# ScalarE copies the causal mask into the score banks of a latent attention

## The chip, the cores and the metric

The kernel runs on one core of one Trainium2 chip. The metric is the device time of one launch in microseconds, the median of several runs. TensorE (PE) has a weight queue of its own (PEld), and beside it work VectorE (DVE), ScalarE (ACT), GpSimd (POOL) and the DMA queues, of which SyncE (SP) issues most. Each engine runs its own program in order and meets the others only in semaphores.

## The reference, cut to what matters

The program computes one layer: a cross attention of 16x64 query rows to 16x1601 context rows, a relative attention, then a latent attention and a mixture of experts. The change is in the latent attention (`mla`), which runs over 16 sequences of 64 tokens with 16 heads:

```
kk = concat([k, k_rope]);  qq = concat([q, q_rope])          # 16 + 16 values a head
scores = einsum('bqhd,bkhd->bhqk', qq, kk) * scale
causal = tril(ones((S, S)))
scores = where(causal, scores, finfo.min)
probs  = softmax(scores)
y      = einsum('bhqk,bkhd->bqhd', probs, v) @ W_o
```

## The kernel before, in words

The 1024 tokens are eight blocks of 128 rows, two sequences each. A block has 16 heads x 64 keys of scores a row, which fill two PSUM banks: bank 4 for heads 0 to 7 (half f=0) and bank 5 for heads 8 to 15 (f=1).

The blocks are pipelined by hand in `self_step(k)`, which every engine has in its own version. The steps k=1 to 4 stand in a hardware loop, and 0, 5, 6 and 7 are written out. In step k TensorE works on four blocks at once, in this order: it transposes the queries of block k+1 (`query_columns`, L905), the first half of block k's weights (`weight_columns`, L940), makes the latents of block k+2 (`latents`, L872), transposes the keys of block k+1 (`key_columns`, L905) and the second half of the weights (L940), makes the rotary keys (L878), then the scores of block k+1 for f=0 (`self_scores`, L924 and L930), the output of block k (`self_output`, L950), the products from the latents of block k+2 (L882, L885, L898), the scores for f=1 (L924 and L930), transposes of block k+3 (L863) and the output product of block k (L960 to L962). Steps 6 and 7 have no further blocks to make latents of.

`self_scores` starts each half with one bf16 product of an identity (`ident_bf`) and the mask (`causal_bf`, eight copies of a 64-column mask, 0 or -1e30), 128 rows x 512 columns, which begins the sum in the bank. Four products of queries and keys add to it; each writes one half of the partitions (`bank[4 + f][own, ...]`). The mask product waits until the exponentials of the block before have read the bank (`sexp_ready`), and the products of queries and keys wait for the spread keys (`kTh_ready`).

ScalarE's `self_step(k)` moves the queries' columns out (`queries_columns_out`, L1608), the first half of the transposed weights (`weights_out`, L1628), spreads two of four parts of the keys (`keys_spread`, two copies, L1391), takes the eight exponentials of f=0 (`self_exps`, L1621), moves out what came from the latents (`heads_out`, L1594 to L1602), and takes the eight exponentials of f=1. In step 0 the order is keys_spread, weights_out, and then one cast of an expert's weights (L1657). VectorE spreads the other two parts of the keys (L1391, DVE), moves out the second half of the weights, splits two pieces of expert weights in the loop's steps (L2191), and takes the negated row maximum of each half (`self_max`, L2161 and L2163), on which the exponentials wait. Between the two maxima lie the casts of the attention's output (L2177, L2179), the norm of a later block and one reciprocal (`self_inv`, L2169). GpSimd multiplies the exponentials with the reciprocal sums (L1287).

Two more places are touched. In the relative attention, GpSimd clears `hn4` (L1262) and later `pos_g` (L1268); VectorE's first `group_turned` waited for the first of these, `attT_cleared`. The mask tile is made by VectorE long before (L2072).

Of the kernel before, what the change touches and what calls it, by code (L numbers as in the profile page):

```python
# [128 lines left out]
def perceiver_kernel(nc, x, ctx_keys, consts, vecs, rows, Wq, Wv, Wr, Wout, Wkvd, Wqd, Wku, Wqu, Wvu, Wropeq, Wropek,  # L129
                     Wo, Wexp, Wrouter, out):  # L130
    with ExitStack() as ctx:
        def sem(name):
            return ctx.enter_context(nc.semaphore(name))

        def sbuf(scope, name, shape, dt=F32):
            return scope.enter_context(nc.sbuf_tensor(name, shape, dt))
# [3 lines left out]
        bank = [ctx.enter_context(nc.psum_tensor(f"bank{i}", [P, 512], F32)) for i in range(8)]  # L140
# [16 lines left out]
        ident_bf = sbuf(ctx, "ident_bf", [P, P], BF16)  # L157
# [5 lines left out]
        hn4 = sbuf(ctx, "hn", [P, 4, D])  # L163
# [30 lines left out]
        def place(kb, name, shape, dt=F32):  # L194

            with ExitStack() as below:
                if kb:
                    sbuf(below, f"{name}_below", [P, int(kb * 256)])
                return sbuf(below, name, shape, dt)
# [47 lines left out]
        causal_bf = place(151, "causal_bf", [P, 8, SQ], BF16)  # L247
# [67 lines left out]
        pos_loaded = sem("pos_loaded")  # L315
        hg_act, hg_dve, ku_ready, v_full, v_out, con_full, con_out = (sem(n) for n in ("hg_act", "hg_dve", "ku_ready", "v_full", "v_out", "con_full", "con_out"))
        abias_ready, exp_ready, ainv_ready, att_ready = (sem(n) for n in ("abias_ready", "exp_ready", "ainv_ready", "att_ready"))
        attT_cleared, pos_cleared, attT_ready, o_full, o_act, o_dve = (
            sem(n) for n in ("attT_cleared", "pos_cleared", "attT_ready", "o_full", "o_act", "o_dve"))
        ohi_ready, olo_ready = sem("ohi_ready"), sem("olo_ready")  # L320
        bout_added, y2_full, y2_ready = sem("bout_added"), sem("y2_full"), sem("y2_ready")

        mla_loaded, raw_loaded = sem("mla_loaded"), sem("raw_loaded")
        causal_ready, cleared, xn_ready, xnT_full, xnT_ready = (sem(n) for n in ("causal_ready", "cleared", "xn_ready", "xnT_full", "xnT_ready"))
        lat_full, lat_ready, k_full, vv_full, q_full = (sem(n) for n in ("lat_full", "lat_ready", "k_full", "vv_full", "q_full"))
        raw_ready, vv_ready, kq_ready, qTh_full, kTh_full = (sem(n) for n in ("raw_ready", "vv_ready", "kq_ready", "qTh_full", "kTh_full"))
        qTh_ready, kTh_ready, self_full, sbias_ready, sexp_ready = (sem(n) for n in ("qTh_ready", "kTh_ready", "self_full", "sbias_ready", "sexp_ready"))
# [47 lines left out]
        def own_values(t, half):  # L375

            at = slice(0, 34 * HD) if half == 0 else slice(HD, 31 * HD)
            blocks = t[SQ * half:SQ * (half + 1), at].rearrange("p (b r d) -> p b r d", b=2, d=HD)
            return blocks[:, :, 0:2 * PAIRS - 1:2, :]
# [167 lines left out]
        def _(pe):  # L547
# [370 lines left out]

            def self_scores(t, par, halves):
                for f in halves:  # L920
                    if not (isinstance(t, int) and t == 0):
                        pe.wait_ge(sexp_ready, 2 * t + f - 1)

                    nc.tensor.matmul(bank[4 + f][:], ident_bf[:], causal_bf[:].rearrange("p n q -> p (n q)"), start=True,  # L924
                                     stop=True)
                    pe.wait_ge(kTh_ready, 2 * t + 2)
                    for i in range(2):
                        for b in range(2):
                            own = slice(SQ * b, SQ * (b + 1))
                            last = nc.tensor.matmul(bank[4 + f][own, i * D // 2:(i + 1) * D // 2], qT_h[par][:, 2 * f + i, own],  # L930
                                                    kT_h[par][:, 2 * f + i, 4 * b:4 * b + 4, :].rearrange("p n q -> p (n q)"),
                                                    start=False, stop=True, skip_group_check=True)
                    last.then_inc(self_full, 1)
# [154 lines left out]
            for j in range(NJ):  # L1088
# [13 lines left out]
                elif j == 4:  # L1102
# [5 lines left out]
                    for k in range(1, NT):  # L1108
                        nc.tensor.matmul(bank[3][:, k * NE:NT * NE], ones_bf[:], picks[:, 0:(NT - k) * NE], start=False,
                                         stop=True, skip_group_check=True)  # L1110

                    for k in range(NT):
                        last = nc.tensor.matmul(bank[3][:, NT * NE:(NT + 1) * NE], ones_bf[:], r_picks[:, k, :], start=k == 0,
                                                stop=k == NT - 1, skip_group_check=True)
# [92 lines left out]
            with pe.Fori(0, TILES // 2 - 2) as i:  # L1207
                at = places_of(2 * i + 2, 3)
                for n, par in enumerate((1, 0)):
                    t = 2 * i + 4 - par  # L1210
# [17 lines left out]
        def _(pool):  # L1228
# [30 lines left out]
            nc.gpsimd.tensor_tensor(y[:], y[:], bout_sb[:].unsqueeze(1).broadcast_to([P, NT, D]),  # L1259
                                    ALU.add).then_inc(bout_added, 1)  # L1260
            pool.wait_ge(hT_full, NT)
            nc.gpsimd.memset(hn4[:], 0.0).then_inc(attT_cleared, 1)  # L1262
            pool.wait_ge(kT_act, NH)
            pool.wait_ge(kT_dve, NH)
            group_queries(0, 0)
# [123 lines left out]
        def head_keys_out(copy, par, h):  # L1389
            rows_h = slice(HD * h, HD * (h + 1))  # L1390
            return copy(kT_h[par][rows_h, :, KEY_PLACES[h], :], bank[3][rows_h, :].rearrange("p (c b q) -> p c b q", c=QUADS, b=2))  # L1391

        @block.scalar
        def _(act):
# [194 lines left out]
            def heads_out(k, par):  # L1589
                act.wait_ge(k_full, k + 1)  # L1590
                kr = bank[2][:].rearrange("p (a h d) -> p a h d", a=2, d=RD)
                if not (isinstance(k, int) and k == 0):
                    act.wait_ge(kq_ready, k)
                nc.scalar.copy(raw[:, 0:HEADS, :], kr[:, 0])  # L1594
                nc.scalar.copy(kq[par][:, 0:HEADS, 0:RD], kr[:, 1])
                act.wait_ge(q_full, k + 1)
                qr = bank[1][:].rearrange("p (a h d) -> p a h d", a=2, d=RD)
                nc.scalar.copy(kq[par][:, HEADS:, 0:RD], qr[:, 0])
                nc.scalar.copy(raw[:, HEADS:, :], qr[:, 1]).then_inc(raw_ready, 1)
                act.wait_ge(vv_full, k + 1)  # L1600
                for half in range(2):
                    last = nc.scalar.copy(own_values(v_own[par], half),  # L1602
                                          bank[3][SQ * half:SQ * (half + 1), :].rearrange("p (b r d) -> p b r d", b=2, d=HD))
                last.then_inc(vv_ready, 1)

            def queries_columns_out(k, par):
                act.wait_ge(qTh_full, k + 1)
                nc.scalar.copy(qT_h[par][:].rearrange("p c q -> p (c q)"), bank[3][:]).then_inc(qTh_ready, 1)  # L1608

            def keys_spread(k, par):  # L1610
                act.wait_ge(kTh_full, k + 1)
                for h in range(2):
                    last = head_keys_out(nc.scalar.copy, par, h)
                last.then_inc(kTh_ready, 1)

            def self_exps(k, par, halves):
                for f in halves:
                    act.wait_ge(sbias_ready, 2 * k + f + 1)
                    for n in range(8):
                        h = 8 * f + n  # L1620
                        last = nc.scalar.activation(sp_[par][:, h, :], bank[4 + f][:, n * SQ:(n + 1) * SQ], ACT.Exp,  # L1621
                                                    bias=s_bias[par][:, h:h + 1], scale=SELF_SCALE,
                                                    accum_out=s_sum[par][:, h:h + 1])
                    last.then_inc(sexp_ready, 1)

            def weights_out(k):
                act.wait_ge(spT_full, 2 * k + 1)
                nc.scalar.copy(spT[:, 0:4, :].rearrange("p n q -> p (n q)"), bank[6][:]).then_inc(spT_act, 1)  # L1628

            def self_step(k, par, scores=True, project=True):  # L1630
                first = isinstance(k, int) and k == 0
                if scores and not first:
                    queries_columns_out(k + 1, 1 - par)
                if first:
                    keys_spread(1, 1)
                weights_out(k)
                if scores and not first:
                    keys_spread(k + 1, 1 - par)
                elif not scores:
                    expert_columns_out(0)  # L1640
                    expert_columns_out(1)
                    for t in range(4):
                        columns_high(t)
                if isinstance(k, int) and k == 0:
                    act.wait_ge(raw_loaded, 4 * 16)
                    high_part(up)
                if scores:
                    self_exps(k + 1, 1 - par, (0,))
                if project:
                    heads_out(k + 2, par)  # L1650
                if scores:
                    self_exps(k + 1, 1 - par, (1,))
# [12 lines left out]
            def columns_high(k):  # L1665
                act.wait_ge(xf_act if k < 2 else xf_ready, k + 1 if k < 2 else k - 1)
                nc.scalar.copy(xT_hi[:, :, k * P:(k + 1) * P], xf[k % 4][:]).then_inc(xhi_ready, 1)
# [7 lines left out]
            queries_columns_out(0, 0)  # L1675
            keys_spread(0, 0)
            heads_out(1, 1)
            self_exps(0, 0, range(2))
            self_step(0, 0)
            with act.Fori(0, NT // 2 - 2) as i:  # L1680
# [96 lines left out]
        def _(dve):  # L1777
# [253 lines left out]
            group_low(3, 1)  # L2031
            group_max(1, 1)
            group_inv(0, 0)
            dve.wait_ge(attT_cleared, 1)
            group_turned(0, 0)
            for g in range(NG - 2):
                group_max(g + 2, g % 2)
# [422 lines left out]
            with dve.Fori(0, TILES // 2 - 1) as i:  # L2460
                for par in range(2):
                    t = 2 * i + 1 + par
# [48 lines left out]
```

## Time and profile before

| | |
|---|---|
| median of 3 runs | 825.94 us (825.93 to 828.04) |
| the profiled execution | 827.49 us |
| its span, first to last instruction | 825.7 us |
| mean granted TensorE clock | 0.997 of full |
| TensorE busy | 792.1 us |
| VectorE, ScalarE, GpSimd busy | 523.7, 311.3, 301.0 us |

The times are device microseconds. Of the profiled execution 1.8 us lie outside the span. A row of the timeline gives the start, the duration, the engine, the source line, what it writes and reads, the shapes and the number of instructions merged, and in brackets the idle time before it with what ended it. TensorE's products are pipelined, so the distance from one start to the next tells more than the duration. An fp32 product shows as two or more records.

### The profile page before, as it was taken

Reading aid. Unit: us, or ns where it says so; the run is one execution under the profiler, and the core shown is the slowest. Engines: PE = TensorE matmul, PEld = TensorE weight load, DVE = VectorE, ACT = ScalarE, POOL = GpSimd, SP = SyncE. Lnnn points to the kernel's source line nnn. Section 1 sums busy time; section 2 is a strip of 40 time slices with the busy share of each in tenths; the row PEclk is TensorE's granted clock in tenths of the full one; section 3 lists DMA queues with packets and bytes.
Section 4 is the critical chain, followed back from the end, with each engine's and each line's share of the span. In section 5 each row is a group of like instructions: output and inputs, shape, how many; then the busy total and the mean of one; then the engine's idle time right before and its main releaser. Section 6 shows DMA issues by size and latency. Waiting matters only on the chain.

```text
span 825.7 us, 16716 instructions
## 1 busy us (share of the span) xinstructions
PE 792.1 (96%) x6414; PEld 582.8 (71%) x6415; DVE 523.7 (63%) x1175; ACT 311.3 (38%) x827; POOL 301.0 (36%) x157
## 2 busy tenths in 40 slices
PE   4899999999989999999999999999999999999996
PEld 3555455555547778878876777688888888888883
DVE  5879777977755346776788877855473433343334
ACT  4312331233153427853267756723422112211211
POOL 0000000000062843543022222443639999993033
PEclk9999999999999999999999999999999999999999
DMA  9968556855502013040189000040475464541147
GB/s 342 382 238 319 201 207 234 319 205 208 211 32 103 1 51 106 3 128 7 53 287 375 3 0 0 2 153 1 178 275 204 159 203 155 185 143 51 55 119 259
DMA packets 46573, 127.00 MB, mean 154 GB/s; under 512 B 4001, under 2 KB 8353, under 8 KB 40369
## 3 DMA queue, kind: packets, MB, share of 16 engines
q1 hardware_dynamic: 36752, 105.44, 35.1%
q10 hardware_dynamic: 7200, 12.32, 4.3%
q0 software_dynamic: 2560, 8.39, 3.1%
q8 instruction: 44, 0.72, 0.4%
q14 instruction: 17, 0.13, 0.0%
HBM read 101.99 MB, written 24.15 MB: 153 GB/s over the span
## 4 chain that ended last, share of the span: by engine, by line
PE 78%; DVE 8%; DMA 6%; POOL 3%; ACT 2%; issue 2%; SPq 1%; another core or an unknown queue 0%; DVEq 0%; ACTq 0%; POOLq 0%
PE scores L592 11%; PE bank L625 8%; PE bank L1128 7%; PE bank L1130 7%; PE bank L1129 6%; DMA nat<-in_ctx_keys 5%; DVE ctxT L1820 2%; PE bank L682 2%; POOL picked L1370 2%; PE bank L836 2%; PE bank L684 2%; PE bank L683 2%; PE bank L842 2%; PE bank L837 2%; PE bank L872 2%
## 5 line engine op out<-in xcount | busy, mean ns | idle before, releaser
L1820 DVE STREAM_TRANSPOSE ctxT<-nat 128x1024 f32<-128x1024 f32 (+3 forms) x124 | 116.9, 1005 | 4.1 <-DMA nat<-in_ctx_keys 3.7
L625 PE MATMUL bank<-nat,probT 128*64 128x512 f32 (+1 forms) x416 | 94.4, 597 | 0.1
L592 PE MATMUL scores<-ctxT,hn 32*64 32x385 f32 (+5 forms) x2048 | 88.6, 487 | 3.5 <-DVE ctxT L1820 2.5
L1235 POOL TENSOR_TENSOR wq_lo<-wq_raw,wq_hi 128x1024 fp32r<-128x1024 f32 x4 | 9.5, 2402 | 223.3 <-ACT wq_hi L1461 223.3
L1357 POOL TENSOR_TENSOR ring_lo<-ring_raw,ring_hi 128x2048 fp32r<-128x2048 f32 x18 | 83.0, 4612 | 15.1 <-ACT ring_hi L1708 14.0
L592 PEld LDWEIGHTS scores<-ctxT,hn 32*64 32x64 f32 x2048 | 65.1, 131 | 24.2 <-issue 12.9
L1128 PE MATMUL bank<-ring_hi,xg_lo 128*128 x180 | 74.2, 412 | 0.4 <-DVE xg_lo L2440 0.4
L1130 PE MATMUL bank<-ring_hi,xg_hi 128*128 x180 | 70.6, 392 | 0.0
L1129 PE MATMUL bank<-ring_lo,xg_hi 128*128 x180 | 70.1, 389 | 0.0
L625 PEld LDWEIGHTS bank<-nat,probT 128*64 128x64 f32 (+1 forms) x416 | 28.8, 136 | 52.9 <-issue 51.4
L2452 DVE TENSOR_TENSOR rhm_lo<-bank,rhm_hi 128x512 fp32r<-128x512 f32 x21 | 14.5, 693 | 79.5 <-ACT rhm_hi L1719 75.9
L1725 ACT COPY hn<-bank 128x512 f32<-128x512 f32 x22 | 12.9, 587 | 113.8 <-PE bank L1130 106.9
L1355 POOL TENSOR_TENSOR ring_hi<-ring_raw,cst 128x2048 fp32r<-128x2048 f32 x15 | 54.1, 3604 | 0.0
L1621 ACT ACTIVATE sp<-bank,s_bias 128x64 f32<-128x64 f32 x128 | 38.1, 326 | 21.7 <-DVE s_bias L2163 21.6
L1287 POOL TENSOR_TENSOR sp<-sp,s_inv 128x512 f32<-128x512 f32 x16 | 16.8, 1051 | 80.2 <-DVE s_inv L2169 80.2
L1397 ACT ACTIVATE qn<-y,nmr,rstd 128x2048 f32<-128x2048 f32 x8 | 16.8, 2094 | 61.7 <-DVE nmr L1882 61.7
L1130 PEld LDWEIGHTS bank<-ring_hi,xg_hi 128*128 128x128 f32 x180 | 33.8, 188 | 7.8
L2435 DVE TENSOR_SCALAR xg_hi<-bank,vec 128x128 fp32r<-128x128 f32 x88 | 24.8, 346 | 21.8 <-PE bank L1138 21.5
L1128 PEld LDWEIGHTS bank<-ring_hi,xg_lo 128*128 128x128 f32 x180 | 33.9, 188 | 6.2 <-issue 0.6
L1129 PEld LDWEIGHTS bank<-ring_lo,xg_hi 128*128 128x128 f32 x180 | 34.0, 189 | 5.9
L1370 POOL DMA_INDIRECT picked<-y_slots,slots x16 | 15.8, 986 | 50.3 <-POOLq L1364 44.2
L1128 PE MATMUL bank<-ring_hi,rhm_lo 128*128 x84 | 32.8, 390 | 0.0
(310 smaller groups left out, 1881.4 us busy)
## 6 DMA issues: line engine op xcount, KB each, us to landing
nat<-in_ctx_keys SPq DMA_DIRECT2D x48, 1024.0 KB, 7.6
ring_raw<-in_Wexp SPq DMA_DIRECT2D x21, 1024.0 KB, 6.2
x_slots<-zeros SPq DMA_DIRECT2D x1, 5632.0 KB, 17.6
y_slots<-zeros SPq DMA_DIRECT2D x1, 5632.0 KB, 32.3
hn<-x_slots ACTq DMA_DIRECT2D x22, 256.0 KB, 4.2
y_slots<-hn ACTq DMA_DIRECT2D x22, 256.0 KB
w_raw<-in_Wexp SPq DMA_DIRECT2D x3, 1024.0 KB, 5.3
nat<-in_ctx_keys SPq DMA_DIRECT2D x16, 130.0 KB
```

Of the source, the lines that this page charges most:

```text
L592: last = nc.tensor.matmul(scores4[64 * b:64 * b + 64, i, 0:keys_in[i]], q4[rows_i, j, 64 * b:64 * b + 64], ctxT[rows_i, b, j, 0:keys_in[i] ...
L625: last = nc.tensor.matmul(bank[7][64 * b:64 * b + 64, :], probT[0:n, j, 64 * b:64 * b + 64], nat[k % 2][0:n, b, j, :], start=j == 0, stop= ...
L1128: nc.tensor.matmul(b[:], x_lo[:, c, :], hi, start=c == 0, stop=False)
L1129: nc.tensor.matmul(b[:], x_hi[:, c, :], lo, start=False, stop=False)
L1130: last = nc.tensor.matmul(b[:], x_hi[:, c, :], hi, start=False, stop=c == HC - 1)
L1287: nc.gpsimd.tensor_tensor(sp_[par][:, at, :], sp_[par][:, at, :], s_inv[par][:, at].unsqueeze(2).broadcast_to([P, 8, SQ]), ALU.mult).then_ ...
L1355: nc.gpsimd.tensor_tensor(ring_hi[at], ring_raw[at], zero, ALU.add).then_inc(split_hi, 1)
L1357: last = nc.gpsimd.tensor_tensor(ring_lo[at], ring_raw[at], ring_hi.bitcast(F32)[at], ALU.subtract)
L1370: nc.gpsimd.indirect_dma_start(picked[2 * k + i][:], None, y_slots, bass.IndirectOffsetOnAxis(slots[:, k, i:i + 1], 0)).then_inc(picked_lo ...
L1621: last = nc.scalar.activation(sp_[par][:, h, :], bank[4 + f][:, n * SQ:(n + 1) * SQ], ACT.Exp, bias=s_bias[par][:, h:h + 1], scale=SELF_SCALE,
L1820: dve.transpose(dst, src).then_inc(columns_ready, 1)
L2435: last = dve.tensor_scalar(xg_hi[par][:, c, :], columns[c], weights[c], None, ALU.mult)
```

## The change

For blocks 1 to 7, ScalarE copies the mask into bank 4 and bank 5 (`scores_seeded`), each after its own exponentials have read the bank, and TensorE's products of queries and keys add to what stands there. The 14 mask products of these blocks are gone; TensorE waits for `seeded` in their place. In ScalarE's step the two copies stand after weights_out and before keys_spread (in step 0: before keys_spread, which stands first). Block 0 keeps its two mask products. ScalarE gets a wait for the mask tile ahead of its first exponentials. A semaphore is given up: VectorE's first `group_turned` waits for `pos_cleared`, the later of the two clearings.

```
             def self_scores(t, par, halves):
                 for f in halves:
-                    if not (isinstance(t, int) and t == 0):
-                        pe.wait_ge(sexp_ready, 2 * t + f - 1)
-
-                    nc.tensor.matmul(bank[4 + f][:], ident_bf[:], causal_bf[:].rearrange("p n q -> p (n q)"), start=True,
-                                     stop=True)
+                    if isinstance(t, int) and t == 0:
+                        nc.tensor.matmul(bank[4 + f][:], ident_bf[:], causal_bf[:].rearrange("p n q -> p (n q)"), start=True,
+                                         stop=True)
+                    else:
+                        pe.wait_ge(seeded, 2 * t + f - 1)
                     pe.wait_ge(kTh_ready, 2 * t + 2)
...
-            nc.gpsimd.memset(hn4[:], 0.0).then_inc(attT_cleared, 1)
+            nc.gpsimd.memset(hn4[:], 0.0)
...
+            def scores_seeded(k):
+                for f in range(2):
+                    act.wait_ge(sexp_ready, 2 * k + f + 1)
+                    nc.scalar.copy(bank[4 + f][:], causal_bf[:].rearrange("p n q -> p (n q)")).then_inc(seeded, 1)
+
...
                 if first:
+                    scores_seeded(k)
                     keys_spread(1, 1)
                 weights_out(k)
                 if scores and not first:
+                    scores_seeded(k)
                     keys_spread(k + 1, 1 - par)
...
             heads_out(1, 1)
+            act.wait_ge(causal_ready, 1)
             self_exps(0, 0, range(2))
...
-            dve.wait_ge(attT_cleared, 1)
+            dve.wait_ge(pos_cleared, 1)
             group_turned(0, 0)
```

## Rows read from the trace of the kernel before

**Rows 1.** The page: each engine's busy time, and the chain that ended last.
```profile
PE 792.1 (96%) x6414; PEld 582.8 (71%) x6415; DVE 523.7 (63%) x1175; ACT 311.3 (38%) x827; POOL 301.0 (36%) x157
...
PE 78%; DVE 8%; DMA 6%; POOL 3%; ACT 2%; issue 2%; SPq 1%; another core or an unknown queue 0%; DVEq 0%; ACTq 0%; POOLq 0%
```
**Rows 2.** Busy time by stretch: PE, PEld, DVE, ACT, POOL, clock, DMA share, GB/s.
```profile
455.50:470.20 14.70, 14.70 (x121) 11.05 (x120) 12.11 (x27) 9.28 (x43) 3.31 (x3) 1.00 0.00 0
...
612.00:792.00 180.00, 179.61 (x868) 148.50 (x867) 72.92 (x203) 38.71 (x64) 135.97 (x33) 1.00 0.43 145
```
**Rows 3.** Timeline of TensorE in step 2, around both halves of the scores.
```profile
463.34 1.89 PE L878 MATMUL bank<-wrk_sb,xnT 128*128 128x256 f32 x8
465.07 0.38 PE L924 MATMUL bank<-causal_bf,ident_bf 128*128 128x512 bf16 x1
465.38 1.08 PE L930 MATMUL bank<-kT_h,qT_h 128*64 128x256 f32 x8
466.29 1.10 PE L950 MATMUL bank<-spT,v_own 128*64 128x64 f32 x32
...
467.86 1.02 PE L885 MATMUL bank<-wq_up,latT 128*128 128x512 f32 x2
468.81 1.08 PE L898 MATMUL bank<-wvu_sb,latT 128*64 128x256 f32 x8
469.83 0.39 PE L924 MATMUL bank<-causal_bf,ident_bf 128*128 128x512 bf16 x1
470.15 1.08 PE L930 MATMUL bank<-kT_h,qT_h 128*64 128x256 f32 x8
```
**Rows 4.** Timelines of ScalarE and VectorE in the same step.
```profile
463.11 1.16 ACT L1391 COPY kT_h<-bank 32x512 f32<-32x512 f32 x2 [1.67 <-PE bank L905]
...
472.21 0.31 ACT L1621 ACTIVATE sp<-bank,s_bias 128x64 f32<-128x64 f32 x1 [0.20 <-DVE s_bias L2163]
...
463.12 1.40 DVE L1391 COPY kT_h<-bank 32x512 f32<-32x512 f32 x2
...
465.16 1.28 DVE L2191 TENSOR_TENSOR w_lo<-w_raw,w_hi  x2
...
471.28 0.69 DVE L2161 TENSOR_REDUCE s_max<-bank 128x8 f32<-128x512 f32 x1 [0.80 <-PE bank L930]
```
**Rows 5.** Timelines of TensorE and ScalarE in step 0.
```profile
436.04 0.38 PE L924 MATMUL bank<-causal_bf,ident_bf 128*128 128x512 bf16 x1
436.35 1.08 PE L930 MATMUL bank<-kT_h,qT_h 128*64 128x256 f32 x8
...
433.93 1.15 ACT L1391 COPY kT_h<-bank 32x512 f32<-32x512 f32 x2
...
438.42 0.31 ACT L1621 ACTIVATE sp<-bank,s_bias 128x64 f32<-128x64 f32 x1 [0.94 <-DVE s_bias L2163]
```
**Rows 6.** Timelines of VectorE, ScalarE and TensorE in steps 5 and 6.
```profile
510.62 0.69 DVE L2161 TENSOR_REDUCE s_max<-bank 128x8 f32<-128x512 f32 x1 [0.45 <-PE bank L930]
...
518.96 0.59 ACT L1608 COPY qT_h<-bank 128x512 f32<-128x512 f32 x1 [0.23 <-PE bank L905]
519.44 0.59 ACT L1628 COPY spT<-bank 128x512 f32<-128x512 f32 x1
520.29 1.16 ACT L1391 COPY kT_h<-bank 32x512 f32<-32x512 f32 x2 [0.26 <-PE bank L905]
...
521.75 1.08 PE L930 MATMUL bank<-kT_h,qT_h 128*64 128x256 f32 x8 [0.67 <-DVE kT_h L1391]
...
523.88 0.31 ACT L1621 ACTIVATE sp<-bank,s_bias 128x64 f32<-128x64 f32 x1 [2.42 <-DVE s_bias L2163]
```
**Rows 7.** The one instruction that made the mask tile (source line L2072).
```profile
L2072 DVE CAST causal_bf<-cst x1: 2015/2015/2015, 371.6 to 371.6; 128x512 bf16<-128x512 f32 x1
```
**Rows 8.** GpSimd's second clearing (timeline), and VectorE's turns (source line L2017).
```profile
302.09 1.81 POOL L1268 MEMSET pos_g<- 128x2048 f32 x1 [1.26 <-PE bank L776]
...
L2017 DVE STREAM_TRANSPOSE hn<-att x32: 431/435/443, 317.0 to 364.0; 32x256 f32<-32x256 f32 x32
```

More of the change, by code:

```diff
@@ L317, in perceiver_kernel @@
         abias_ready, exp_ready, ainv_ready, att_ready = (sem(n) for n in ("abias_ready", "exp_ready", "ainv_ready", "att_ready"))
-        attT_cleared, pos_cleared, attT_ready, o_full, o_act, o_dve = (
-            sem(n) for n in ("attT_cleared", "pos_cleared", "attT_ready", "o_full", "o_act", "o_dve"))
+        pos_cleared, attT_ready, o_full, o_act, o_dve = (
+            sem(n) for n in ("pos_cleared", "attT_ready", "o_full", "o_act", "o_dve"))
         ohi_ready, olo_ready = sem("ohi_ready"), sem("olo_ready")
@@ L323, in perceiver_kernel @@
         mla_loaded, raw_loaded = sem("mla_loaded"), sem("raw_loaded")
+        seeded = sem("seeded")
         causal_ready, cleared, xn_ready, xnT_full, xnT_ready = (sem(n) for n in ("causal_ready", "cleared", "xn_ready", "xnT_full", "xnT_ready"))
```

## The prediction, made before the changed kernel ran

> **What bounds the kernel now.** I read the page first, then the busy time by stretches, then the timelines of the latent attention engine by engine. On the page TensorE is busy for 96% of the span and carries 78% of the chain that ended last; ScalarE has 38% and 2% [rows 1]. So a product taken from TensorE can be worth its time, and a copy given to ScalarE can be free, if both hold in the stage in question. In a middle step of the latent attention they do: TensorE is busy for 14.70 of 14.70 us at the full granted clock, VectorE for 12.11 and ScalarE for 9.28, with no transfer running [rows 2]. The step repeats every 14.68 us, and the chain of waits runs through TensorE alone there. The routed experts behind it have TensorE busy for 179.61 of 180 us [rows 2]; their weight loads and GpSimd's scatters are released by TensorE's own products. What the latent attention gains should therefore reach the end whole.
>
> **What TensorE no longer does.** The mask product occupies the time between its start and that of the next product: 465.38 - 465.07 = 0.31 us for f=0 and 470.15 - 469.83 = 0.32 us for f=1 [rows 3]. The change of form around it counts too. Products that write half the partitions (128\*64) follow each other cheaply: four of them take 0.91 us from start to start when such products come next (465.38 to 466.29), but 1.02 when the full-width mask product comes next (468.81 to 469.83) [rows 3]. The other way, from full to half width, costs about 0.09: L885's two records of 512 columns should stream in 0.86 by L878's pace (1.73 us for eight records of 256), and take 0.95 up to L898 [rows 3].
>
> - f=0 today: L878 to the mask 1.73, mask 0.31, together 2.04. Without it: 1.73 + 0.09 = 1.82. Gain 0.22.
> - f=1 today: L898 to the mask 1.02, mask 0.32, together 1.34. Without it half width follows half width: 0.91. Gain 0.43.
>
> That is 0.65 us a step. The lower bound is that both changes of form still cost what they do, so that only the 0.22 of streaming goes, twice: 0.44. The upper is 0.31 + 0.43 = 0.74. I take 0.65, since rows show each of these successions.
>
> **What ScalarE does more.** Two copies of 128x512 from SBUF to PSUM a step. The trace has none in that direction. The nearest row is the copy of 128x512 from PSUM to SBUF, 0.59 us, whose successor starts 0.48 later [rows 6]; I take 0.48 each, 0.96 for the pair. The bounds: 0.4 below (no row of 512 columns on ScalarE is spaced much closer), 0.6 above (nothing overlapped). Copies among the exponentials show no table load. The Trainium skill, page "ScalarE: Activation LUTs", section "What ACT_TABLE_LOAD costs", gives 186 ns + 0.833 ns a column with 93 ns of overlap: an estimate by that page is 0.52 us from one copy to the next, and the sum would end 0.08 us later for each place where the pair is exposed. The row for the other direction has 0.48; the same page calls PSUM the quicker destination, which no row of before shows.
>
> In a middle step ScalarE sits idle for 1.67 us just where the copies go, until the keys' columns come [rows 4]. So 0.96 hides there with 0.7 to spare. Even later keys would be covered first: ScalarE's spread takes 1.16 against VectorE's 1.40, and VectorE's ends at 464.52, while TensorE could use the keys at 463.34 + 1.82 = 465.16 [rows 3, 4]. Two copies may thus take 1.67 + 0.24 + 0.6 = 2.5 us before TensorE waits. ScalarE is free from 463.11 - 1.67 = 461.44, so both banks are seeded by 462.4, and the new wait of TensorE is met 2.7 us early.
>
> **What is late next in a middle step.** VectorE's row maximum of f=0 already comes right after its weight pieces (465.16 + 1.28 = 466.44), so it stays where it is relative to the step's start. The maximum of f=1 has 0.80 of idle before it, ended by the scores [rows 4]; with the scores 0.65 earlier, 0.15 is left. Everything from there to the next step's queries hangs on that maximum and moves with it. ScalarE's exponentials of f=1 had only 0.20 of idle before them [rows 4], so they move by about 0.2, not 0.65, but nobody on TensorE waits for them until the second half of the weights in the next step; the copy of the queries is then some 0.1 late and TensorE uses it 2 us later. So the four loop steps (blocks 2 to 5) give 4 x 0.65 = 2.6 us.
>
> **Step 0.** Here the copies stand in front of the keys' spread with nothing to hide behind: ScalarE starts the spread right after its exponentials at 433.93 [rows 5]. It would start at 434.9 and end at 436.05, and the scores of f=0, which could go at 436.04 without the mask, go at about 436.15 instead of 436.35 [rows 5]. Gain 0.2. ScalarE's next exponentials have 0.94 of idle before them, which the 0.96 just uses up. The 0.43 of f=1 meets VectorE's chain (norm and rotation), which hangs on the output of block 0 and moves only by the 0.2. Between 0 and 0.65.
>
> **Steps 5 and 6.** In step 5 the maximum of f=0 waits for the scores (0.45 idle) and moves by 0.22 [rows 6]; ScalarE works without a pause from there to 518.96 - 0.23 = 518.73, and with 0.23 idle before the queries' copy this copy can come 0.49 earlier, at 518.47, where TensorE alone would allow 0.65. Then weights at 518.95, the two masks at 519.43 and 519.91, and the spread of the keys at 520.39 instead of 520.29, ending at 521.55. Now ScalarE, not VectorE, is last, and the scores of f=0 start at 521.60 against 521.75 [rows 6]. From there the path leads over the maximum to the sixteen exponentials from 523.88 on, and TensorE waits for these. So both steps together give 0.15, and the masks removed in blocks 6 and 7 are otherwise lost. At 0.6 a copy this term is -0.1, at 0.4 it is 0.3.
>
> **The rest** costs nothing. `pos_cleared` comes at 303.9, and VectorE's first turn at 317.0, after weights that GpSimd makes later in its own order [rows 8]. The mask tile was ready at 373.6 [rows 7].
>
> **Sum:** 0.2 + 2.6 + 0.15 = 2.95 us. The profiled execution took 827.49 (span 825.7) and would take 824.5 (span 822.75). It stood 1.55 above the median of 825.94; from the median the forecast is 823.0. About 0.3%, 2.5 us, is what a measurement of this kernel can tell from no change, and the forecast lies just beyond that.
>
> **Rivals.**
> - *Only the streaming goes.* The form changes keep their price, wherever they fall: 8 x 0.22 + 0.35 = 2.1, so 823.8. For it: the mask's duration less the form change is 0.22. Against it: half width after half width is seen at 0.91. The Trainium skill, "TensorE: Matmul & The Clock Gate", section "Back-to-back issue gap", puts a product of 512 columns at about 216 ns, which as an estimate gives this same rival. Chance 0.20.
> - *ScalarE or VectorE sets the pace.* A step gains only the 0.20 that stood idle before the exponentials of f=1 [rows 4]: 4 x 0.20 + 0.35 = 1.15, so 824.8. Against it: no product waits for these exponentials within 2 us. Chance 0.09.
> - *Everything comes through.* The copies are much shorter, or the last steps have room that I don't see: 14 x 0.32 = 4.5, so 821.5. Against it: the 0.67 that TensorE waits in step 6 [rows 6]. Chance 0.06.
> - *Slower: the keys come late.* If a copy of this tile cost what its making cost on VectorE, 2.0 us [rows 7], the pair would take 4.0 and exceed the 2.5 of cover by 1.5. Each of five steps would lose 1.5 - 0.65 = 0.85, step 0 2.8 and step 6 3.4: +10, so 836. It decides from 1.2 us a copy on, where the exposed pairs of steps 0 and 6 eat the 2.95. Against it: 0.59 for as many columns on ScalarE itself. Chance 0.05.
>
> **How the numbers follow.** The forecast has 0.60, its own range 822.3 to 823.8 (loop steps 0.44 to 0.74, step 0 0 to 0.65, end -0.1 to 0.3). The range for 8 in 10 runs from 821.9 to 825.2: it takes in the first two rivals and leaves out the other two and the scatter of the runs, which reached 2 us. Faster by over 0.3% needs 2.5 us: 0.8 of the forecast's 0.60, all of the 0.06, a fifth of the first rival's, 0.58. Slower 0.05. The rest, 0.37, is within 0.3%.
>
> **What would show it.** The middle steps repeat every 14.03 us instead of 14.68, with L878 to L930 at 1.82 and L898 to L930 at 0.91. Two ScalarE copies into the banks stand 0.48 apart, with some 0.7 idle left before the keys' spread. The idle time before the maximum of f=1 falls to 0.15. In step 6 the scores of f=0 wait for ScalarE's `kT_h`. I am wrong if L930 is released by the copies in a middle step, if the maximum of f=1 waits for nothing, or if step 6 gains as much as the others.

## The result, and the profile after

The changed kernel took 821.54 us (median of 7 runs, 819.5 to 826.42) against 826.03 (7 runs, 825.39 to 829.42): ratio 0.9946, 95% interval 0.9924 to 0.9967. That is 4.5 us where 2.95 were forecast, and 0.4 us below the range. Its profiled execution took 821.11 us with a span of 819.3, which is 6.4 us less than the profiled one of before. The latent attention accounts for 3.0 of these, as the following shows. Medians and ratios are those of fast runs; one slow run of the kernel before (3378 us, in the series of c_after_2) is left out.

The page after, beside [rows 1]:
```profile
PE 786.1 (96%) x6400; PEld 578.0 (71%) x6401; DVE 522.0 (64%) x1175; ACT 317.9 (39%) x841; POOL 301.2 (37%) x157
```
Fourteen instructions left TensorE and fourteen came to ScalarE, 6.6 us more busy there. A whole middle step, from one block's first scores to the next one's (the columns as in [rows 2]):
```profile
461.51:475.50 13.99, 13.99 (x117) 10.93 (x117) 12.00 (x28) 10.27 (x44) 3.32 (x3) 1.00 0.01 2
```
TensorE is still busy without a gap at the full clock, and the step is 0.69 us shorter (14.68 before). TensorE's timeline of that step answers [rows 3], with all numbers of lines one higher:
```profile
459.69 1.89 PE L879 MATMUL bank<-wrk_sb,xnT 128*128 128x256 f32 x8
461.51 1.08 PE L931 MATMUL bank<-kT_h,qT_h 128*64 128x256 f32 x8
...
464.94 1.08 PE L899 MATMUL bank<-wvu_sb,latT 128*64 128x256 f32 x8
465.86 1.03 PE L931 MATMUL bank<-kT_h,qT_h 128*64 128x256 f32 x8
466.82 0.66 PE L864 MATMUL bank<-cst,hn 128*128 128x128 f32 x4
```
From L879 to the scores of f=0 it is 1.82 us (2.04 before), from L899 to those of f=1 0.92 (1.34 before), and 0.96 from there to the transposes, which took 1.01 before (470.15 [rows 3] to 471.16). ScalarE and VectorE in the same step, against [rows 4]:
```profile
457.66 1.12 ACT L1630 CAST bank<-causal_bf 128x512 f32<-128x512 bf16 x2
459.45 1.16 ACT L1392 COPY kT_h<-bank 32x512 f32<-32x512 f32 x2 [0.67 <-PE bank L906]
...
466.94 0.69 DVE L2170 TENSOR_REDUCE s_max<-bank 128x8 f32<-128x512 f32 x1 [0.33 <-PE bank L931]
```
The copies (the record's CAST x2) stand where ScalarE was idle, and 0.67 of its 1.67 us is left. Before the maximum of f=1 0.33 of the 0.80 is left, still ended by the scores. Steps 0 and 6 are the exposed ones. ScalarE in step 0, then TensorE and ScalarE in step 6, against [rows 5, 6]:
```profile
431.06 1.14 ACT L1630 CAST bank<-causal_bf 128x512 f32<-128x512 bf16 x2
432.10 1.16 ACT L1392 COPY kT_h<-bank 32x512 f32<-32x512 f32 x2
...
513.51 1.15 ACT L1630 CAST bank<-causal_bf 128x512 f32<-128x512 bf16 x2
514.55 1.16 ACT L1392 COPY kT_h<-bank 32x512 f32<-32x512 f32 x2
...
515.85 1.08 PE L931 MATMUL bank<-kT_h,qT_h 128*64 128x256 f32 x8 [1.02 <-ACT kT_h L1392]
```
Here the reader sees the copies directly ahead of the keys' spread with no pause, and TensorE held by ScalarE's `kT_h` for 1.02 us, where it had waited 0.67 for VectorE's [rows 6].

**Where the 6.4 us are.** I divide the span at two starts on TensorE's timeline: the first product of queries and keys, and the last group L960 of the latent attention (L961 after). This table is worked out from those two starts and the span of each profile.

| profile | until the first scores | latent attention | the rest | span |
|---|---|---|---|---|
| before | 426.7 | 110.4 | 288.6 | 825.7 |
| before, run again (c_before) | 424.0 | 110.4 | 289.1 | 823.5 |
| before, run again (c_before_2) | 425.5 | 110.4 | 289.4 | 825.3 |
| after | 423.8 | 107.4 | 288.1 | 819.3 |
| after, run again (c_after) | 425.0 | 107.4 | 288.5 | 820.9 |
| after, run again (c_after_2) | 422.5 | 107.4 | 286.7 | 816.6 |
| after, run again (c_after_3) | 424.9 | 107.3 | 288.6 | 820.8 |

The middle column hardly scatters, and differs by 3.0 us. The first scatters by 2.7 us with the kernel before alone, and the third by 1.9 us with the changed kernel alone. A good part of the first column's scatter arises within the first 31 us, in the loads of the cross attention: ScalarE's second cast of queries starts at 30.87 in the trace of before and at 28.43 in c_before, the same program.
```profile
28.43 2.09 ACT L1397 ACTIVATE qn<-y,nmr,rstd 128x2048 f32<-128x2048 f32 x1 [10.18 <-DVE nmr L1882]
```
In the changed kernel it starts at 28.53, and in c_after at 30.00. So neither value belongs to one kernel. A second part arises between 220 and 240 us, where the granted clock is 0.91 in six of these seven profiles and 1.00 in c_after_2, the one whose first stretch is the shortest. The third column's 286.7 is 1.8 us below c_after's 288.5, and 1.0 of that arises in the loop over the routed experts: from its first product to its last it takes 200.0 us in c_after_2 and 200.7 to 201.0 in the other six.

### The profile page after: what moved, and what is told of

Read it like the earlier page. It is cut to its first block, busy times and chain, and to the rows that moved or that the text cites. A ratio compares the mean times of both kernels' runs of the same rounds, so it can differ in the third digit from the quotient of the medians.

```text
span 819.3 us, 16715 instructions
## 1 busy us (share of the span) xinstructions
PE 786.1 (96%) x6400; PEld 578.0 (71%) x6401; DVE 522.0 (64%) x1175; ACT 317.9 (39%) x841; POOL 301.2 (37%) x157
## 4 chain that ended last, share of the span: by engine, by line
PE 80%; DVE 8%; DMA 3%; POOL 3%; ACT 3%; issue 2%; SPq 0%; another core or an unknown queue 0%; DVEq 0%; ACTq 0%; POOLq 0%
PE scores L593 11%; PE bank L626 10%; PE bank L1129 7%; PE bank L1131 7%; PE bank L1130 7%; DMA nat<-in_ctx_keys 3%; PE bank L683 2%; POOL picked L1371 2%; DVE ctxT L1829 2%; PE bank L837 2%; PE bank L685 2%; PE bank L838 2%; PE bank L843 2%; PE bank L684 2%; PE bank L873 2%
## 5 line engine op out<-in xcount | busy, mean ns | idle before, releaser
L593 PEld LDWEIGHTS scores<-ctxT,hn 32*64 32x64 f32 x2048 | 62.3, 131 | 25.9 <-issue 14.9
L1734 ACT COPY hn<-bank 128x512 f32<-128x512 f32 x22 | 12.9, 587 | 113.7 <-PE bank L1131 106.9
```

The costliest lines, as they stand in the source:

```text
L593: last = nc.tensor.matmul(scores4[64 * b:64 * b + 64, i, 0:keys_in[i]], q4[rows_i, j, 64 * b:64 * b + 64], ctxT[rows_i, b, j, 0:keys_in[i] ...
```

## Experiments

**The two kernels unchanged, and the semaphores alone.** c_before, c_before_2, c_after, c_after_2 and c_after_3 are the kernels as they are. e_sem_only is the kernel before with:
```
-            nc.gpsimd.memset(hn4[:], 0.0).then_inc(attT_cleared, 1)
+            nc.gpsimd.memset(hn4[:], 0.0)
...
-            dve.wait_ge(attT_cleared, 1)
+            dve.wait_ge(pos_cleared, 1)
...
             heads_out(1, 1)
+            act.wait_ge(causal_ready, 1)
```


> The kernel before, unchanged. It tells how much of the 4.5 us between the medians is scatter. Theory (the change itself is worth 3.05 us, all in the latent attention, and the rest of the 6.4 us between the two profiled spans comes from the cross attention by chance): the stretch from the first score product of the latent attention to the end is 399.0 us within 0.5, as in the trace of before, whatever the stretch ahead of it takes (426.7 there), and the median lies within 1.5 us of 826. Rival (the change also speeds up what runs ahead of it, for good): the stretch ahead is again 426 to 427 here, and 424 in the other runs with the change.

> The changed kernel, unchanged. Theory: from the first score product of the latent attention to the end 395.5 us within 0.5, as in its first trace (819.3 - 423.8); the stretch ahead falls anywhere between 423 and 428; the median is 2.5 to 4.5 below the kernel before of the same chip. Rival (a lasting gain ahead of the latent attention): the stretch ahead is again within 0.5 of 423.8, and the gain is 6 us by the profiles.

> The semaphores alone: the kernel before with the given-up semaphore, the wait for the later clearing and the wait for the mask tile; all mask products stay on TensorE and nothing is copied by ScalarE. Theory: no difference, ratio 1.000 within 0.002, 399.0 us from the first score product to the end, VectorE's first turn still released by the weights. Rival (the edit ahead of the latent attention brings the 2.9 us seen there): 823 us.

> The changed kernel once more. The change has two readings so far, 4.5 us (7 runs) and 3.1 us (12 runs). Theory (3.0 us, the rest scatter of the first 31 us of the kernel): ratio 0.9963 within 0.0015, 107.4 us from the first score product to the start of the last output product. Rival (the first reading was right): 0.9946.

> The kernel before, once more, beside the next run on the same chip. Theory: ratio 1.000 within 0.0015, the latent attention's stretch 110.4 us.

> The changed kernel, a fourth reading of its size (4.5, 3.1 and 5.2 us so far). Theory (3.0 us, all of it in the stretch of 107.4 against 110.4 us, and scatter besides): ratio 0.9963 within 0.0015. Rival (about a microsecond more comes from outside that stretch): 0.995 or below, and the stretches ahead or behind shorter than in the kernel before of the same chip.

| kernel | runs, median | ratio to before (95%) |
|---|---|---|
| c_before | 12, 826.66 | 1.0004 (0.9990 to 1.0019) |
| c_before_2 | 12, 825.46 | 0.9986 (0.9966 to 1.0006) |
| e_sem_only | 12, 825.48 | 0.9990 (0.9972 to 1.0007) |
| c_after | 12, 823.52 | 0.9963 (0.9946 to 0.9979) |
| c_after_2 | 8, 820.54 | 0.9945 (0.9924 to 0.9967) |
| c_after_3 | 12, 823.00 | 0.9949 (0.9929 to 0.9970) |

The semaphores do nothing: latent attention 110.5 us, the other two stretches as in the kernel before (424.4 and 288.7), and an interval that holds 1. The four readings of the change lie between 0.9945 and 0.9963, and every interval holds 0.9964, which is 3.0 us. But c_after_2 missed my 0.9963 within 0.0015, and c_after_3 lies at its edge. Both read what I had written for the rivals (0.9946, and 0.995 or below), and in c_after_3 the stretches ahead and behind are 0.6 and 0.8 us shorter than in c_before_2, as its rival had it. Against the unchanged kernel that ran in the same series, c_after is 3.1 us below c_before and c_after_3 2.5 below c_before_2. Two of the three kernels that keep all mask products also read 0.8 to 1.2 us below the reference runs around them, though nothing in their profiles is shorter for good. I take the change for 3.0 us, which the stretch shows in each of four profiles. The total may hold more. The four readings, each against all runs of the kernel before in its series and weighted by their scatter, give a difference of the means of 3.7 us, 3.1 to 4.3. That interval counts each run as independent, and kernels that keep all mask products read up to 1.2 us apart. In the profiles the rest behind the latent attention took 288.6 to 289.4 us with the kernel before and 286.7 to 288.6 with the changed one, but 289.4 in e_loop_only and 288.9 in e_f1_only, which have most of the change. So up to a microsecond more is neither shown nor excluded, and its cause stays open.

**No mask at all.** e_nomask leaves the causal mask out for blocks 1 to 7: no mask product and no copy, and the first of the two products on each half of the partitions begins the sum.
```
-                        pe.wait_ge(seeded, 2 * t + f - 1)
+                        pe.wait_ge(sexp_ready, 2 * t + f - 1)
...
-                                                    start=False, stop=True, skip_group_check=True)
+                                                    start=not (isinstance(t, int) and t == 0) and i == 0, stop=True, skip_group_check=True)
...
-                    nc.scalar.copy(bank[4 + f][:], causal_bf[:].rearrange("p n q -> p (n q)")).then_inc(seeded, 1)
+                    pass
```


> Leaves the causal mask out for blocks 1 to 7: no mask product on TensorE, no copy on ScalarE; the first product of queries and keys begins the sum. It prices the mask itself. From the first score product to the start of the last output product the kernel before took 110.4 us and the changed kernel 107.4. Theory (the copies cost nothing in steps 1 to 5 and are exposed in steps 0 and 6): steps 1 to 5 repeat every 14.00 us as in the changed kernel, step 0 gives 0.3 and step 6 0.45 more, 106.7. Rival (the copies also cost in the middle steps): the period falls below 13.9 and the stretch below 106.

The latent attention took 106.9 us, and the middle step 13.99, the same as with the copies:
```profile
464.97 1.08 PE L931 MATMUL bank<-kT_h,qT_h 128*64 128x256 f32 x8
...
478.96 1.08 PE L931 MATMUL bank<-kT_h,qT_h 128*64 128x256 f32 x8
```
So ScalarE's copies are free in the middle steps and cost 0.4 in all at the two ends, 0.3 less than I had expected of them: step 6 is 11.97 without them and 12.37 with them. (The one timed execution, 831.89 us, is no price of the mask. The rest took 295.8 us there; I put that down to the other values that reach the router, which no run shows.)

**How much cover there is.** e_twice makes each copy twice, e_thrice three times, each after the last has ended:
```
-                        pe.wait_ge(seeded, 2 * t + f - 1)
+                        pe.wait_ge(seeded, 2 * (2 * t + f - 1))              # 3 * in e_thrice
...
-                    nc.scalar.copy(bank[4 + f][:], ...).then_inc(seeded, 1)
+                    for r in range(2):                                       # 3 in e_thrice
+                        if r:
+                            act.wait_ge(seeded, 2 * (2 * k + f) + r)         # 3 * in e_thrice
+                        nc.scalar.copy(bank[4 + f][:], ...).then_inc(seeded, 1)
```


> Each seed copy is made twice, the second after the first has ended: two more copies a step on ScalarE, an estimated 1.3 us more (0.59 each and a semaphore). The cover left in a middle step of the changed kernel is 0.67 idle before the keys' spread, 0.24 by which VectorE's spread is longer, and 0.64 until TensorE uses the keys: 1.55. Theory: the period stays 14.00, steps 0 and 6 lose 1.3 each, 107.4 becomes 110.0. Rival (ScalarE's order sets the pace, every copy counts): 7 x 1.3 more, 116.5.

> Each seed copy is made three times: an estimated 2.6 us more a step. Theory (cover of 1.55 in a middle step): five middle steps lose 1.05 each, the period is 15.05, and TensorE's first score product waits for ScalarE's spread of the keys; steps 0 and 6 lose 2.6 each; 107.4 becomes 117.8. Rival (the cover is larger, as the step has slack elsewhere): period below 14.3, about 113. Rival (no cover at all): 125.

With two copies the middle step stays at 13.99, as forecast; with three it is 14.93 (466.94 to 481.87), and TensorE waits for ScalarE's keys, as in this row of e_thrice's timeline:
```profile
466.94 1.08 PE L931 MATMUL bank<-kT_h,qT_h 128*64 128x256 f32 x8 [0.85 <-ACT kT_h L1392]
```
That is 0.94 more a step where 1.05 was expected. So the cover of some 1.6 us beyond the pair is right, and the limit for the pair is about 2.6 us (2.5 in the prediction). The rival in which every copy counts is refuted. The whole stretch came out at 111.2 for e_twice and 120.2 for e_thrice, where I had 110.0 and 117.8. Steps 0 and 6 lost 1.3 each in e_twice as expected. The other 1.3 comes behind step 6, and the busy time by stretches of e_twice shows how:
```profile
516.90:520.80 3.90, 1.31 (x8) 0.84 (x8) 2.83 (x7) 3.73 (x7) 2.15 (x2) 1.00 0.00 0
520.85:524.50 3.65, 3.65 (x43) 3.09 (x45) 1.02 (x3) 0.87 (x6) 0.00 (x0) 0.54 0.02 4
```
TensorE stood idle for 2.31 us before block 7's scores (and twice for 0.30 just before), and then ran at a granted clock of 0.54, near the lower level of 1.2 GHz, for the next 3.6 us; the scores' records took 1.75 us where they take 1.08. In the changed kernel the idle time there is 1.02 us, and the clock stays at 1.00. In e_thrice the same happens behind both written-out steps, after 2.59 us of idle time in step 0 and 3.56 in step 6:
```profile
435.85:440.00 4.15, 4.15 (x48) 3.50 (x50) 1.64 (x4) 3.85 (x13) 0.00 (x0) 0.59 1.03 390
526.74:531.00 4.26, 4.26 (x44) 3.33 (x46) 1.40 (x3) 1.25 (x9) 0.00 (x0) 0.50 0.00 0
```
There the period from block 1 to 2 lost 2.1 us where 1.05 was expected, and the part behind step 6 lost 1.8 where no loss was expected. Each of e_nomask, e_twice, e_thrice and e_f1_only was timed once, so the stretches of their profiles are all they show.

**One half alone.** In e_f1_only only bank 5 is seeded, and f=0 keeps its product:
```
-                    if isinstance(t, int) and t == 0:
+                    if f == 0 or isinstance(t, int) and t == 0:
+                        if not (isinstance(t, int) and t == 0):
+                            pe.wait_ge(sexp_ready, 2 * t + f - 1)
...
-                        pe.wait_ge(seeded, 2 * t + f - 1)
+                        pe.wait_ge(seeded, t)
...
-                for f in range(2):
+                for f in (1,):
```


> Only bank 5 (f=1) is seeded by ScalarE; f=0 keeps its mask product in all blocks. Theory (a product's worth depends on its neighbours: 0.43 between half-width products, 0.22 after a full-width one): middle steps repeat every 14.22 us, 14.68 less about 0.45; the stretch from the first score product to the last output product is 107.4 + 5 x 0.22 less what one exposed copy fewer saves in steps 0 and 6 (0.2 and 0.3): 108.0. Rival (each product is worth its own 0.32): a period of 14.35.

```profile
461.09 1.89 PE L879 MATMUL bank<-wrk_sb,xnT 128*128 128x256 f32 x8
463.13 1.08 PE L933 MATMUL bank<-kT_h,qT_h 128*64 128x256 f32 x8
...
477.33 1.08 PE L933 MATMUL bank<-kT_h,qT_h 128*64 128x256 f32 x8
```
The step is 14.20 or 14.21 us, and the latent attention 108.1. So removing the f=1 product was worth 0.48 of the 0.69 and the f=0 product 0.21, though the two products are the same instruction. By these rows the product between two half-width groups costs more; that it pays for two changes of form is my reading of the distances (1.34 to 0.92 from L898 or L899 on, 1.01 to 0.96 behind the scores), and no run tests another order.

**Products where TensorE waits anyway.** e_loop_only gives blocks 1 and 7 their products back (step 0 then copies nothing either, and TensorE waits for two copies fewer), e_last_product block 7 alone:
```
-                    if isinstance(t, int) and t == 0:
+                    if isinstance(t, int) and t in (0, NT - 1):     # (0, 1, NT - 1) in e_loop_only
+                        if t:
+                            pe.wait_ge(sexp_ready, 2 * t + f - 1)
...
-                    scores_seeded(k)
+                    if not (isinstance(k, int) and k == NT - 2):
+                        scores_seeded(k)
```


> ScalarE seeds the banks for blocks 2 to 6 alone; blocks 1 and 7 (steps 0 and 6) have their mask products back on TensorE, where it waits for the keys anyway. Theory: the copies of steps 0 and 6 stand exposed in front of the keys' spread, so without them the scores of block 7 start 0.35 us earlier relative to the rest, while the product of f=0 hides in the wait and that of f=1 costs TensorE time that the exponentials of f=0 cover. From the first score product to the end 395.2 against 395.5. Rival (every removed product counts, at 0.32 to 0.34 each): four products come back, 396.8.

> The changed kernel with the mask of block 7 alone back on TensorE; ScalarE copies nothing in step 6. Theory (in step 6 the copies stand before the keys' spread and make ScalarE last there, the scores of f=0 start 8.02 us after those of f=1 before them and 7.56 where the product is back): 107.4 becomes 107.0, the f=1 product of 0.32 costs nothing since the exponentials of f=0 cover it. The ratio cannot tell 0.4 us from nothing: 0.9958 within 0.0015. Rival (each product on TensorE costs its time): 108.0.

The latent attention took 107.1 and 106.9 us, ratios 0.9955 (0.9938 to 0.9972) and 0.9935 (0.9910 to 0.9961), whose distance from the change's own the runs can't tell. Two of my expectations missed by what lies outside the latent attention: e_loop_only took 396.5 us from the first scores to the end where I had 395.2 (and the rival 396.8), as its rest took 289.4, and e_last_product's ratio is below my 0.9958 by more than the 0.0015. The stretch is what refutes the rivals, which would have it at 108.0 or above. In e_last_product block 7's first scores start 519.44 - 511.90 = 7.54 us after block 6's second, against 515.85 - 507.83 = 8.02 in the changed kernel, and are released by VectorE again:
```profile
519.44 1.08 PE L933 MATMUL bank<-kT_h,qT_h 128*64 128x256 f32 x8 [0.32 <-DVE kT_h L1394]
...
521.39 0.39 PE L925 MATMUL bank<-causal_bf,ident_bf 128*128 128x512 bf16 x1
521.71 1.08 PE L933 MATMUL bank<-kT_h,qT_h 128*64 128x256 f32 x8
```
The product at 521.39 costs TensorE 0.32 us and the kernel nothing: from block 7's first scores to the last output product it is 15.36 us, against 15.35 in the changed kernel. By the stretch this is the best version, 0.5 below the change and 3.5 below the kernel before.

## Why the prediction was right in its working and wrong in its range

By the starts of each block's first scores, the 3.04 us of the latent attention fall like this. The forecast is the prediction's, sorted into the same sections (the 0.15 of steps 5 and 6 is 0.22 for block 6's f=0, which ends the fourth period, less 0.07):

| section | before | after | saved | forecast |
|---|---|---|---|---|
| block 0 to 1 (step 0) | 9.68 | 9.59 | 0.09 | 0.2 |
| block 1 to 2 | 14.35 | 14.12 | 0.23 | 0.22 |
| blocks 2 to 6, four periods | 58.72 | 55.96 | 2.76 | 2.6 |
| block 6 to 7 (step 6) | 12.33 | 12.37 | -0.04 | -0.07 |
| block 7 to the last output product | 15.35 | 15.35 | 0 | 0 |

- *The value of a product.* 0.22 for f=0 and 0.43 for f=1 came out at 0.22 and 0.42, and e_f1_only shows the difference by itself. The period fell by 0.69, not 0.65: half width followed by L864 came out 0.05 cheaper too, which I hadn't counted. This term, 2.76 for 2.6 us, is the largest miss of the sum.
- *ScalarE's copy.* I took 0.48 from one to the next. The pair takes 1.12 with records of 0.61, so 0.51 from the first to the second; in steps 0 and 6 the spread starts 1.04 after the pair, 0.52 a copy. The estimate of 0.52 by the Trainium skill, page "ScalarE: Activation LUTs", section "What ACT_TABLE_LOAD costs", was the nearer. The same page's remark that PSUM is the quicker destination (section "Step-by-step: what each stage is for") has no support here: 0.61 into PSUM from SBUF (with a change from bf16 to f32), 0.59 the other way (f32 on both sides).
- *The cover in a middle step.* Right, and shown by e_nomask, e_twice and e_thrice.
- *What is late next.* The maximum of f=1 stays with the scores. 0.33 is left before it, where I had 0.15. I had misread the maximum of f=0, which before starts here:
```profile
466.51 0.69 DVE L2161 TENSOR_REDUCE s_max<-bank 128x8 f32<-128x512 f32 x1
```
  That is 1.35 us after the start of the weight pieces (465.16 [rows 4]), and 1.13 after the scores of f=0, as the maximum of f=1 is after its scores (470.15 to 471.28 [rows 3, 4]). So it did wait for the scores. Now it follows the weight pieces by 1.20, and VectorE comes forward by the 0.15.
- *Step 0 and step 6.* The mechanism was right (ScalarE last with the keys, the exponentials on the path); step 0 was 0.1 too high, as the longer copies would have it. Step 6 hit by two misses that cancel: counted from block 6's first scores, ScalarE's queries' copy came 0.20 earlier than forecast (9.07 us after them, 9.27 forecast), while the copies and the release of the scores took 0.17 longer. By the prediction's own terms that copy could come 0.45 earlier (0.22 + 0.23), not 0.49. Its range had a slip too: the bounds given for the three terms add up to 1.7 to 3.9 us, 822.0 to 824.3, not to 822.3 to 823.8.
- *The rest.* Nothing behind the latent attention gave the gain back. Whether it added to it stays open.

**The step that failed** is the last of the prediction's working: "leaves out the other two and the scatter of the runs, which reached 2 us". The range ended at 821.9 because it held mechanisms alone. The sum itself held: the terms came to 3.04 us where it had 2.95. What it gave no room to is all that happens outside the latent attention. The cross attention's first 31 us alone moved the kernel before by 2.4 us between two of its profiles, and 33 runs of the kernel before within one series reached from 824.0 to 829.3, with a standard deviation of 1.5. An estimate from these: the difference of two medians of seven such runs has a standard error of about 1 us, so 4.5 was within reach of a change worth 3.0, and the measured interval, 0.9924 to 0.9967, holds it. The rival "everything comes through" (4.5 us, 821.5) fits the first reading within 0.1 us and is refuted in its mechanism: with the four products of blocks 1 and 7 back on TensorE the latent attention takes 107.1 us (e_loop_only), not more than the 107.4 without them, and the stretch shows 3.0. The first reading's other 1.5 us are thus outside what the change does in the latent attention. Most of it can be scatter; the mean of all readings, 3.7 us, leaves 0.7 whose cause stays open.

## What to carry to other kernels

Price a removed product by its neighbours, from the distance between starts with and without such a neighbour: here the same instruction was worth 0.21 or 0.48 us. Work moved to another engine is free only as far as that engine idles just there, so look at each step of a pipeline, the written-out first and last ones above all, and leave the work where the old engine waits anyway. And where a gain is a third of a per cent, divide the span at two instructions around the change: the stretch told 3.0 us from one profile each, when medians of 7 to 12 runs said anything from 2.5 to 5.0. Such a stretch says nothing of what a change does outside it, so look at the other stretches too.

## What the hardware showed unexpectedly

After a wait of 2.31 us on TensorE, behind two of 0.30 (e_twice), the granted clock was 0.54 for the following 3.6 us, so that the wait cost another 1.3 us after its end: 16.6 us instead of 15.35 from block 7's scores to the last output product. After 2.59 and 3.56 us (e_thrice) it was 0.59 and 0.50. With 1.02 us of idle time in the same place, or 0.85 us in every step (e_thrice), the clock stayed at 1.00.
